# Attention scores from 32-partition strips on TensorE's row groups, with operands written to device memory and read back

## The reference

```python
q = (x @ wq).reshape(B, T, H, D); lat = x @ w_down
k = (lat @ wk_up).reshape(B, T, H, D); v = (lat @ wv_up).reshape(B, T, H, D)
q, k = _apply_rope(q, cos, sin), _apply_rope(k, cos, sin)
scores = jnp.einsum('bqhd,bkhd->bhqk', q, k) * scale
pages = jnp.arange(T) // PAGE_SIZE                    # pages of 32 tokens
allowed = pages[None, :] <= pages[:, None]
attn = jax.nn.softmax(jnp.where(allowed, scores, finfo.min), axis=-1)
out = jnp.einsum('bhqk,bkhd->bqhd', attn, v).reshape(B, T, E) @ wo
...
# experts: each token goes to its best 2 of 8, hidden width 256
y = t + sum of w[t, e] * (silu(t @ ew1[e] + eb1[e]) @ ew2[e] + eb2[e])
```

## Time and profile before

| | us |
|---|---|
| median of 3 runs | 585.58 |
| lowest, highest | 583.09, 585.88 |
| profiled execution | 584.54 |
| its span | 582.7 |
| TensorE busy | 499.0 |
| VectorE busy | 387.7 |
| ScalarE busy | 333.9 |
| GpSimd busy | 136.7 |

### The profile page before, as it was taken

The page is one execution under the profiler, slowest core; times in us unless marked ns, Lnnn a source line. Parts: engine busy times, 40 slices in busy tenths (PEclk is TensorE's granted clock), DMA queues, the critical chain, the costliest instruction groups (busy, mean ns, idle before and its releaser), DMA issues.

```text
span 582.7 us, 9046 instructions
## 1 busy us (share of the span) xinstructions
PE 499.0 (86%) x3223; PEld 327.8 (56%) x3223; DVE 387.7 (67%) x704; ACT 333.9 (57%) x504; POOL 136.7 (23%) x143
## 2 busy tenths in 40 slices
PE   3489997997699878999999999999999987778891
PEld 1256654554356444686776866767767554345450
DVE  4888585897577756836556675557674777568871
ACT  2065573654365435577876767767768543335870
POOL 3120000007664764000000000000001466553620
PEclk9767997999999997999999999999999987789997
DMA  6842216112222322748367263474222225523443
GB/s 176 282 96 102 74 37 165 29 29 82 79 75 61 92 74 65 212 128 238 112 166 190 50 183 100 104 197 118 72 66 59 67 63 161 144 64 101 117 114 90
DMA packets 64676, 64.60 MB, mean 111 GB/s; under 512 B 11096, under 2 KB 48088, under 8 KB 64120
## 3 DMA queue, kind: packets, MB, share of 16 engines
q1 hardware_dynamic: 53616, 47.89, 30.3%
q0 software_dynamic: 4096, 8.40, 5.3%
q10 hardware_dynamic: 6920, 7.74, 4.3%
HBM read 32.27 MB, written 21.24 MB: 92 GB/s over the span
## 4 chain that ended last, share of the span: by engine, by line
PE 65%; DVE 12%; ACT 7%; issue 5%; another core or an unknown queue 4%; DMA 4%; SPq 2%; POOL 1%; ACTq 0%; DVEq 0%; POOLq 0%
PE ring L610 13%; PE wide L650 10%; PE ring L630 9%; PE ring L705 6%; DVE row_max L946 6%; PE ring L695 5%; PE ring L569 4%; ACT probs L807 3%; PE ring L633 3%; PE ring L618 2%; PE ring L662 2%; PE ring L634 2%; PE ring L686 2%; PE ring L560 1%
## 5 line engine op out<-in xcount | busy, mean ns | idle before, releaser
L807 ACT ACTIVATE probs<-ring 128x768 f32<-128x768 f32 (+1 forms) x192 | 164.6, 880 | 147.1 <-PE ring L634 65.9
L946 DVE TENSOR_REDUCE row_max<-ring 128x4 f32<-128x512 f32 (+2 forms) x192 | 195.4, 1042 | 79.3 <-PE ring L610 46.2
L610 PE MATMUL ring<-k_head,q_stack 108*128 108x256 f32 (+2 forms) x512 | 132.8, 373 | 27.1 <-issue 10.9
L1142 POOL DMA_INDIRECT pair_in<-y_rows,place x64 | 62.5, 976 | 265.8 <-PE wide L650 245.2
L610 PEld LDWEIGHTS ring<-k_head,q_stack 108*128 108x128 f32 x512 | 80.6, 203 | 63.6 <-issue 30.1
L1129 POOL DMA_INDIRECT slot_rows<-xn,place x64 | 62.8, 981 | 133.5 <-PE wide L650 109.2
L650 PE MATMUL wide<-probs,v_cols 128*32 128x512 f32 (+3 forms) x1024 | 93.2, 461 | 0.8 <-ACT probs L807 0.8
L630 PE MATMUL ring<-q_stack,k_head 128*128 128x512 f32 (+1 forms) x256 | 82.7, 422 | 13.0 <-ACT probs L807 5.3
L630 PEld LDWEIGHTS ring<-q_stack,k_head 128*128 128x128 f32 x256 | 43.7, 203 | 34.2 <-issue 16.0
L650 PEld LDWEIGHTS wide<-probs,v_cols 128*32 128x32 f32 x1024 | 24.2, 111 | 36.4 <-issue 27.6
L798 ACT ACTIVATE k_head<-k_stack,hmask 128x512 fp32r<-128x512 f32 x64 | 40.8, 712 | 6.5 <-DMA k_stack<-roped_lo 5.4
(11 more groups left out here) (123 smaller groups left out, 500.1 us busy)
## 6 DMA issues: line engine op xcount, KB each, us to landing
area<-w_pack SPq DMA_DIRECT2D x39, 321.0 KB, 3.1
area<-slot_rows SPq DMA_DIRECT2D x39, 128.0 KB, 3.4
y_rows<-work SPq DMA_DIRECT2D x39, 128.0 KB, 2.7
slot_rows<-pair_in ACTq DMA_DIRECT2D x4, 1024.0 KB, 6.0
k_stack<-roped_hi SPq DMA_DIRECT2D x64, 64.0 KB
q_stack<-roped_hi SPq DMA_DIRECT2D x64, 64.0 KB
k_stack<-roped_lo SPq DMA_DIRECT2D x32, 64.0 KB
q_stack<-roped_lo SPq DMA_DIRECT2D x32, 64.0 KB
```

What stands on the lines that cost most here:

```text
L610: last = mm(ps[:, at // T, at % T:at % T + width], q_stack[0:MAX0, g, i * P:(i + 1) * P], k_head[0:MAX0, GH * g + r, 0:width], start=True, ...
L807: activation(probs[:, n % 2, 2 * half:2 * half + 2, lo:T], ps[:, :, lo:T], ACT.Exp, scale=SCALE).then_inc(exp_done, 1)
L946: reduce(row_max[:, g, i, heads[0]:heads[-1] + 1], ps[:, :, 0:(i + 1) * P], AX, ALU.max).then_inc(max_done, 1)
L1142: G.indirect_dma_start(pair_in[:, b % 2, which, t * E:(t + 1) * E], None, y_rows, bass.IndirectOffsetOnAxis(ap=place[:, which, at:at + 1], ...
```

## The change

Each head gets its own 32 partitions. A strip holds 24 rows of data (three parts of 8 features), 6 mask rows and 2 rows for the maximum, and four heads lie on the four row groups of TensorE. A score matmul of one head contracts over its 30 or 32 partitions alone. There are no masked copies of the keys, so `heads` and `k_head` are gone. With 6 mask rows a matmul covers two tiles of keys, so the queries 256 to 511 stand twice in a strip, with the mask rows of the upper half in the second copy: a strip of queries is 768 wide.

The rows of a head lie on eight partitions after `split`, and the strips need them in another order. So SyncE writes them to `q_image` and `k_image` in device memory (`write`, nine transfers per batch) and reads them back as strips of 128 partitions (`read`, two transfers per group). There are two sets of strips, for even and odd batches. The constant rows of the images are written once at the start, from masks that VectorE has rounded (`const_ready`), in eleven transfers.

The maxima are made in six jobs per group as before, but each job now has four matmuls of 256 columns for two heads, 24 matmuls per group where there were 16. The transpose of the negated maxima is six tiles of 128 columns, so that they come out on the partitions where the strips have their two rows, with zeros elsewhere; VectorE adds all of it to the strip of queries out of PSUM, and the ScalarE copy and the 16 KB transfer are gone. `o_copy` moves from VectorE to ScalarE. At the end the last four batches of x are fetched into `last_x`, a part of `area`, in place of `k_stack`.

```diff
-MAXIMA = ((0, (0, 1, 2, 3)), (1, (0, 1, 2, 3)), (2, (0, 1)), (2, (2, 3)), (3, (0, 1)), (3, (2, 3)))
+MAXIMA = tuple((tiles, first) for tiles in ((0, 1), (2,), (3,)) for first in (0, 2))
+STRIP = P // GH
+DATA, MASKED, WIDE = 3 * D, STRIP - 2, T + 2 * P
...
-BANKS = {... "neg_max": 1, ...}
+BANKS = {... "neg_max": 2, ...}
-AT = dict(... heads=-1.58, max=-1.71, max_step=0.1, neg=-1.38, pv=0.64,
+AT = dict(... read=-2.2, max=-1.71, max_step=0.1, neg=-1.38, pv=0.64,
+O_COPY = "act"
+SPLIT = ("dve",) * B
...
-        q_stack = sb("q_stack", [P, NG, T], F32R)
-        k_stack = sb("k_stack", [P, NG, T])
-        k_head = sb("k_head", [P, H, T], F32R)
+        q_strip = sb("q_strip", [P, 2, NG, WIDE], F32R)
+        k_strip = sb("k_strip", [P, 2, NG, T], F32R)
-        neg_max = sb("neg_max", [P, NG, TT, MAX_SLOT])
+        neg_max = sb("neg_max", [P, 2, TT, P])
+        q_image, k_image = dram("q_image", (H, STRIP, WIDE)), dram("k_image", (H, STRIP, T))
...
+            def constant(image, rows, cols, from_rows, which, first):
+                n = cols.stop - cols.start
+                source = rounded[from_rows, which, first:first + n].bitcast(F32)
+                sp.dma_start(image[:, rows, cols].rearrange("h x t -> x h t"),
+                             source.unsqueeze(1).to_broadcast([source.shape[0], H, n])).then_inc(image_ready, 16)
+
+            sp.wait_ge(const_ready, 1)
...
+            def write(b, which):
+
+                sp.wait_ge(hi_ready, 2 * b + which + 1)
                 if b >= 1:
+                    for g in range(NG):
+                        sp.wait_ge(strips_in[(b - 1) % 2][g], 32 * ((b - 1) // 2) + 32)
+                hi, lo = roped_hi[:, which, :].bitcast(F32), roped_lo[:, which, :].bitcast(F32)
+                for slot, rows in ((0, hi), (1, hi), (2, lo)) if which else ((0, hi), (2, hi), (1, lo)):
+                    if rows is lo:
+                        sp.wait_ge(lo_ready, 2 * b + which + 1)
+                    at = slice(D * slot, D * slot + D)
+                    if which:
+                        sp.dma_start(k_image[:, at, :], rows).then_inc(k_written, 16)
+                    else:
+                        sp.dma_start(q_image[:, at, 0:T], rows).then_inc(q_written, 16)
+                        sp.dma_start(q_image[:, at, T:WIDE], rows[:, 2 * P:T]).then_inc(q_written, 16)
+
+            def read(b, g):
+
+                if b == g == 0:
+                    sp.wait_ge(image_ready, 16 * NCONST)
+                if b >= 2:
+                    sp.wait_ge(pv_done, NSTEP * (b - 2) + 3 * g + 3)
+                sp.wait_ge(q_written, 96 * b + 96)
+                sp.dma_start(q_strip[:, b % 2, g, :].bitcast(F32),
+                             q_image[GH * g:GH * g + GH].rearrange("h x t -> (h x) t")).then_inc(strips_in[b % 2][g], 16)
+                sp.wait_ge(k_written, 48 * b + 48)
+                sp.dma_start(k_strip[:, b % 2, g, :].bitcast(F32),
+                             k_image[GH * g:GH * g + GH].rearrange("h x t -> (h x) t")).then_inc(strips_in[b % 2][g], 16)
...
             def max_scores(b, m):
-                g, (i, heads) = m // NM, MAXIMA[m % NM]
+                g, (tiles, first) = m // NM, MAXIMA[m % NM]
...
-                width = max(2, i + 1) * P
-                for k, r in enumerate(heads):
-                    at = k * 2 * T // len(heads)
-                    last = mm(ps[:, at // T, at % T:at % T + width], q_stack[0:MAX0, g, i * P:(i + 1) * P],
-                              k_head[0:MAX0, GH * g + r, 0:width], start=True, stop=True)
+                for part in range(2):
+                    i, keys = tiles[part % len(tiles)], slice(0, 2 * P) if tiles[0] == 0 or part == 0 else slice(2 * P, T)
+                    queries = i * P if keys.start == 0 else T + (i - 2) * P
+                    for r in range(2):
+                        rows = slice(STRIP * (first + r), STRIP * (first + r) + MASKED)
+                        last = mm(ps[:, r, 2 * P * part:2 * P * part + 2 * P], q_strip[rows, b % 2, g, queries:queries + P],
+                                  k_strip[rows, b % 2, g, keys], start=True, stop=True)
                 last.then_inc(slot_full, 1)
 
             def neg_max_t(b, g):
                 pe.wait_ge(neg_ready, NG * b + g + 1)
-                ps = take(pe, ("neg_max", b, g))
-                for i in range(TT):
-                    last = turned(ps[0:MAX_SLOT, 0, i * P:(i + 1) * P], neg_max[:, g, i, :], ident[:])
+                ps = take(pe, ("neg_max", b, g)).rearrange("p a t -> p (a t)")
+                for k, i in enumerate((0, 1, 2, 3, 2, 3)):
+                    last = turned(ps[:, k * P:(k + 1) * P], neg_max[:, g % 2, i, :], ident[:])
                 last.then_inc(slot_full, 1)
 
             def scores(b, e):
...
-                    pe.wait_ge(neg_in[g], 16 * b + 16)
+                    pe.wait_ge(neg_rows_ready, NG * b + g + 1)
                 ps = take(pe, ("scores", b, e))
...
+                keys = (j,) if j < 2 else (3, 2)
+                for k, tile in enumerate(keys):
+                    for r in range(2):
+                        rows = slice(STRIP * (2 * half + r), STRIP * (2 * half + r) + STRIP)
+                        to, queries = (slice(j * P, T), slice(j * P, T)) if j < 2 else (slice(2 * P * k, 2 * P * k + 2 * P), slice(T, WIDE))
+                        last = mm(ps[:, r, to], k_strip[rows, b % 2, g, tile * P:(tile + 1) * P],
+                                  q_strip[rows, b % 2, g, queries], start=True, stop=True)
...
+            def o_copy(b, g):
                 if b >= 1:
+                    act.wait_ge(rows_ready, 2 * b)
+                act.wait_ge(pv_done, NSTEP * b + 3 * g + 3)
+                copy(o_cols[:, g, :], wide[g % 2][:]).then_inc(o_done, 1)
...
+            def neg_max_t(b, g):
+                ps = wait_full(dve, ("neg_max", b, g))
+                strip = q_strip[:, b % 2, g, :]
+                tt(strip, strip.bitcast(F32), ps.rearrange("p a t -> p (a t)")[:, 0:WIDE], ALU.add).then_inc(neg_rows_ready, 1)
...
             row_stats(0, 0)
+            dve.wait_ge(s_const, 32)
+            V.tensor_copy(rounded, masks).then_inc(const_ready, 1)
```

206 lines of the change are left out of this document (87 added, 119 removed).

## The result

The changed kernel is slower: 626.58 us median (624.61 to 628.86) against 585.73 us (583.09 to 587.75, four executions where the table ahead has three), a ratio of 1.070 with an interval of 1.065 to 1.076. Two repeats on other chips gave 1.064 (1.056 to 1.071) and 1.063 (1.055 to 1.071). The profiled execution took 628.86 us, its span is 627.0, so 44.3 us more than before's 582.7. Ratios leave out single executions that were over 1.5% slower than the fastest of their kernel; the medians and ranges given hold all of them.

A forecast was written before the change was run, and what follows sets the result against it. TensorE was taken as the bound in the middle third, with VectorE next outside it. TensorE's -40 counted as -27; with VectorE -3, ScalarE -4, device memory +4 and start +3 the sum was -27, giving 558 us, range 530 to 606.

The forecast's parts named there:

- The matmuls (-79): Row-packed maxima and scores: a pair costs one matmul, 2.46 us less in each of 32 groups, -79 us of TensorE.
- the first rival: Weight loads of a row-packed pair queue, so matmuls save only 15 us: 604 us, chance 0.17.
- no overlap: Row-packed matmuls do not run side by side at all, TensorE has 46 us more: 625 us, chance 0.05.
- Regrouping (+35) and transposes (+4): TensorE's changes between matmul forms cost 35 us more; transposes of negated maxima, six per group, 4 us more.
- free regrouping: TensorE's changes of matmul form cost nothing, the 35 us are not paid: 535 us, chance 0.15.
- TensorE in all (-40, to 450 to 465 us busy): Sum of TensorE's terms, -79 + 35 + 4, with its busy time falling from 499.0 to 450 to 465 us.
- Share that reaches the end (0.34 + 0.33): Of TensorE's 40 us, groups in the middle stretch pay in full, the others half: -27 us.
- VectorE takes over: Outside the middle stretch nothing is gained, TensorE's saving counts only -14 us: 571 us, chance 0.15.
- Start (+3): Mask cast and eleven constant transfers put first maxima at 38 to 39 us, not 35.68: +3, bounds -3 and +8.
- Device memory (+4, bounds 0 and 40): Operands going through device memory are late once, in the third batch, and hidden afterwards: +4 us.
- VectorE (379) and ScalarE (294) busy: Busy times after the change: VectorE falls from 387.7 to about 379 us, ScalarE from 333.9 to about 294.
- queued loads: Rival in which a row-packed pair's weight loads do not run side by side: 604 us, chance 0.17.

The follow-up runs named there:

- light: direct with each row maximum taken over a quarter of its keys: 596.36 us, 1.014 of the kernel before.
- lead: direct with reads, maxima and negation due 0.2 of a group's turn earlier: 619.02 us, 1.054 of the kernel before.
- direct: Changed kernel with constants sent straight from device-memory inputs, 16 heads outermost, no VectorE cast: 1.021, 1.045 and 1.028 of the kernel before on three chips.
- slim: Kernel before with every score and maxima matmul's contraction cut to 32 partitions, columns and order kept: 694.6 us, 1.276 of the kernel before.

## Why the prediction was wrong

- **The matmuls (-79).** Right in mechanism: partners start up to 4 ns apart, pairs follow at 0.12 us, and loads don't queue, so the first rival and "no overlap" are out. That the latter's 625 us lies next to the result is chance.
- **Regrouping (+35) and transposes (+4).** At full clock TensorE's work fell by 63.6 us, and -79 + 4 leaves about 11 for the changes of form: a third of the term, near "free regrouping". But a single change isn't free. One from the whole array into the row-packed form costs 0.15 + 0.10 us, about the 0.26 of the prediction, and its 360 changes are there. Counted from start to start at full clock, maxima and scores take 90.5 us less, the transposes 9.6 more and not 4, and all else 17.3 more, together -63.6. Why the changes add up to so little is not shown.
- **TensorE in all (-40, to 450 to 465 us busy).** The failed step: it measured 488.8 us. Durations from the trace of before were used as if its granted clock, 0.938, would stay. 63.6 us at full clock became 10.2 us of busy time. The prediction named the clock only as a thing that would make it wrong, gave it no price and no chance; by TensorE's busy time in half-clock stretches it is +53. Why the clock fell stays open.
- **Share that reaches the end (0.34 + 0.33).** The middle stretch gave 6.7 us, not 0.34 x 40 = 13.6, and there the clock was full in both: 14.3 us of work went, and 7.6 us of waits came. In two more pairs of traces it gave 2.1 us and lost 1.9. In the outer stretches nothing was gained: the rival "VectorE takes over" had this half right. But light shows that it isn't VectorE's time, and that waits on ScalarE grow where those on VectorE shrink. That the hand-offs through the rings of banks are the bound is my reading; lead, which was to test it, didn't bear it out.
- **Start (+3).** Mis-sized: +17.7. Both causes were named, cast and eleven transfers with an outer dimension of three, yet the issues, 0.8 to 3.8 us for one or two, were not priced. Their bound stopped at +8. direct has its first maxima 11 to 14 us earlier.
- **Device memory (+4, bounds 0 and 40).** Right in size: no cost after the first batch shows. The one wait that it put into the third batch isn't there: TensorE waits once for a strip, for the first.
- **VectorE (379) and ScalarE (294) busy.** 371.6 and 296.7, close.

The range ended at 606, in the rival "queued loads"; the start was held to +8 and the clock to nothing. With 15 us more for the start and 53 x 0.67 for the clock the sum would have come to 558 + 15 + 36 = 609, still 18 us short: the waits of the outer stretches are in neither.

## What to carry to other kernels

A row of the trace of before has a duration at the clock that was granted then. Where a change makes TensorE's matmuls narrower or shorter, price the sum once at full and once at half clock in every stretch where TensorE isn't the sole bound. Work taken from the leading engine can come back as waits on the engines it feeds: here 14.3 us less work with the experts gave at most 6.7. And constants written once can hold the issuing queue ahead of everything: price their issues from the trace. Here the long dimension outermost, with a source in device memory, took them from 15 us to between 8 and 10.5.

## What the runs showed of the hardware

- A kernel can stay at half clock with TensorE busy 54.60 of 54.60 us by its records, when all its score matmuls contract over 32 partitions (slim).
- Matmuls on different row groups start up to 4 ns apart, their weight loads 3 ns, and one pair of 256 columns follows another after 0.12 us, as one matmul did before. Behind a matmul on the whole array the first pair is 0.15 us late, and the second another 0.10.
- The same program takes 545.6 us on one chip and 586 to 589 on others, with engines waiting together for up to 10.0 us (DVE row_max L945) on the slower ones while GpSimd gathers or scatters.
- Transfers of constants with two or three rows outermost took up to 3.77 us of SyncE's queue for two issues; with 16 heads outermost and device memory as source 0.6 to 2.3.
